# ScalarE's recurrence program without its loop, and the second extra piece of an attention step behind the values

## The reference, cut to what matters

```
# per expert e (4 of them), per sequence b (4), S = 512, D = 256, 16 heads of 16
q, k, v = split(h @ aiw + aib, 3)
attn = softmax(einsum('bhqd,bhkd->bhqk', q, k) * SCALE)       # 512 x 512 per head
h = einsum('bhqk,bhkd->bhqd', attn, v) ... @ aow + aob
hf = lstm(h, wif, whf, bf); hb = lstm(h[:, ::-1], ...)[:, ::-1]
# lstm, one step of 512:
zg = xt @ Wi + h @ Wh + b;  i, f, g, o = split(zg, 4)
c = sigmoid(f) * c + sigmoid(i) * tanh(g);  h = sigmoid(o) * tanh(c)
```

## Time and profile before

| | us |
|---|---|
| median of three runs | 5555.54 |
| the profiled execution | 5550.52 |
| its span | 5548.7 |
| TensorE busy | 5148.0 (93%) |
| VectorE busy | 4160.4 (75%) |
| ScalarE busy | 2497.2 (45%) |
| GpSimd busy | 1150.2 (21%) |
| attention steps, within the span | about 784 to 2130 |
| recurrence, within the span | about 2236 to 4990 |

### The profile page before, as it was taken

One profiled execution on the slowest core, in us unless ns is written; L12 is line 12 of the kernel. 1 busy time (PEld: TensorE's weight loads), 2 busy tenths in 40 slices (PEclk: granted clock), 3 DMA queues, 4 the chain that ended last, 5 costly groups with the idle time before them and its releaser, 6 DMA issues. The chain is left out here.

```text
span 5548.7 us, 260566 instructions
## 1 busy us (share of the span) xinstructions
PE 5148.0 (93%) x108704; PEld 3567.2 (64%) x108704; DVE 4160.4 (75%) x19277; ACT 2497.2 (45%) x8421; POOL 1150.2 (21%) x5133
## 2 busy tenths in 40 slices
PE   7888879999999997899999999999999999998895
PEld 4545433333333332888888888888888888884442
DVE  4555566666666664999999999999999999991224
ACT  2333446555555553444444444444444444443332
POOL 0000001111111110333333333333333333330000
PEclk9999989999999998999999999999999999999997
DMA  0003354444454443111101111011110111102110
GB/s 13 0 0 104 123 129 85 84 106 103 92 109 84 106 99 137 30 36 25 38 15 38 38 23 38 15 38 38 23 38 20 34 38 23 38 4 88 62 38 12
DMA packets 378077, 300.18 MB, mean 54 GB/s; under 512 B 145993, under 2 KB 357065, under 8 KB 372458
## 3 DMA queue, kind: packets, MB, share of 16 engines
q1 hardware_dynamic: 377886, 298.01, 22.5%
HBM read 178.94 MB, written 119.01 MB: 54 GB/s over the span
## 5 line engine op out<-in xcount | busy, mean ns | idle before, releaser
L1386 PE MATMUL bank<-lparts,lstate 128*32 128x256 bf16 x98304 | 2705.9, 273 | 95.3 <-PEq L1329 46.7
L1386 PEld LDWEIGHTS bank<-lparts,lstate 128*32 128x32 bf16 x98304 | 2455.2, 97 | 346.6 <-DVE lstate L1432 75.1
L1397 DVE STREAM_TRANSPOSE ltz<-bank 128x256 f32<-128x256 f32 x2048 | 920.5, 449 | 8.7 <-PE bank L1386 3.7
L1463 ACT ACTIVATE ltc<-lgc 128x16 f32<-128x16 f32 x2049 | 446.1, 218 | 1013.8 <-DVE lgc L1418 1013.4
L1479 POOL TENSOR_TENSOR wh<-lgate,ltc 128x16 f32<-128x16 f32 x2052 | 471.7, 230 | 1848.6 <-ACT ltc L1463 1777.4
L1114 DVE TENSOR_REDUCE bnegmax<-bank 128x1 f32<-128x512 f32 x1024 | 655.0, 684 | 218.4 <-PE bank L972 218.1
L1458 ACT ACTIVATE lgate<-lz 128x48 f32<-128x48 f32 x2048 | 502.0, 245 | 493.4 <-DVE lz L1408 493.0
L1202 ACT ACTIVATE wh<-bank 128x512 f32<-128x512 f32 x1024 | 554.3, 599 | 368.5 <-PE bank L990 368.2
L1486 POOL COPY ltz<-wh 128x64 f32<-128x64 f32 x2048 | 603.5, 295 | 0.0
L1404 DVE TENSOR_TENSOR lhalf<-ltz 128x128 f32<-128x128 f32 x2048 | 584.1, 285 | 5.0 <-POOL ltz L1486 5.0
L1052 PE MATMUL bank<-xT,bw 128*128 128x512 f32 x1024 | 487.4, 600 | 17.0 <-DVE bzs L1135 16.2
(11 more groups left out here) (211 smaller groups left out, 4712.2 us busy)
## 6 DMA issues: line engine op xcount, KB each, us to landing
zx<-bzs SPq DMA_DIRECT2D x32, 2048.0 KB, 7.3
wh<-zx SPq DMA_DIRECT2D x64, 1024.0 KB, 7.4
qk<-eparts SPq DMA_DIRECT2D x96, 256.0 KB, 2.6
bqp<-qk SPq DMA_DIRECT2D x192, 128.0 KB, 4.9
bkp<-qk SPq DMA_DIRECT2D x192, 128.0 KB, 8.0
hs<-wh SPq DMA_DIRECT2D x32, 512.0 KB, 5.7
cmemT<-hs SPq DMA_DIRECT2D x32, 512.0 KB, 4.2
vx<-evx SPq DMA_DIRECT2D x16, 544.0 KB, 3.7
```

Source lines behind the costliest of these rows:

```text
L1386: last = nc.tensor.matmul(bank[x][32 * q:32 * q + 32, 0:256], top[:, x, e, k].rearrange("p m r -> p (m r)"), parts[:, way, g, k, n, e, q], ...
L1397: nc.vector.transpose(tz[:, x].rearrange("p (n w) -> p n w", w=SLOT)[:, :, 0:32], bank[x][:, 0:256].rearrange("p (n c) -> p n c", n=BLOCKS ...
L1463: nc.scalar.activation(tc[:, x], gc[:, x, 1], ACT.Tanh).then_inc(tanhed[x], 1)
```

## The change

In the attention the second extra piece of a step moves from before `turn_maxima` and `values` to behind them, and `score_t(j - 2, 3)` now stands before `score(j, 3)`. In the recurrence ScalarE's loop over 32 turns of 16 steps is replaced by straight code for all 512 steps; the other engines' loops stay.

```diff
                     if j < HEADS:
                         score(j, 2)
-                        score(j, 3)
                     if 2 <= j < HEADS + 2:
                         score_t(j - 2, 3)
+                    if j < HEADS:
+                        score(j, 3)
+                    if 1 <= j < HEADS + 1:
+                        turn_maxima(j - 1)
+                    if j >= 6:
+                        values((j - 6) // 4, (j - 6) % 4)
                     if at == 0:
                         turn_values(slab, 0)
                     elif at == 1:
...
                     elif end > first + 1:
                         for k in range(KH):
                             product(made, end - 1, k)
-                    if 1 <= j < HEADS + 1:
-                        turn_maxima(j - 1)
-                    if j >= 6:
-                        values((j - 6) // 4, (j - 6) % 4)
...
-PE_STEPS, DVE_STEPS, ACT_STEPS = 4, 8, 16
+PE_STEPS, DVE_STEPS = 4, 8
...
-                with act.Fori(0, S // ACT_STEPS) as turn:
-                    first = ACT_STEPS * turn
-                    for i in range(ACT_STEPS):
-                        for x in range(chains):
-                            tanh_cell((x - 1) % chains, first + (i + (x - 1) // chains))
-                            gates(x, first + i)
+                for t in range(S):
+                    for x in range(chains):
+                        tanh_cell((x - 1) % chains, t + (x - 1) // chains)
+                        gates(x, t)
```

## The result

The changed kernel takes 5467.77 us (median of 4 runs, 5466.13 to 5469.04), the kernel before 5554.57 us (4 runs, 5552.78 to 5557.43): a ratio of 0.9843, 95% interval 0.9826 to 0.9860. That is 86.8 us, or 1.6%, less. The forecast was 5464 us in a range of 5446 to 5492, with 0.93 on faster. The profiled run took 5466.13 us and has a span of 5464.1.

A forecast was written before the change was run, and what follows sets the result against it. TensorE was taken to bound both stages, interrupted by waits on other engines. Attention 46 us plus recurrence 45 us made 91 us, taken from 5555.5 us for a forecast of 5464 us, range 5446 to 5492.

The forecast's parts named there:

- What bounds: Both stages: TensorE bounds attention (busy 1309 of 1346 us) and recurrence (2704 of 2754); the question is what interrupts it.
- ScalarE's turns, 31 at 1.65 us: Recurrence: each turn of ScalarE's 16-step loop costs 1.65 us, so removing 31 gives 51 us.
- GpSimd's turns come up, 6 us: Recurrence: GpSimd's seven late turns, formerly inside ScalarE's 1.65 us, remain and take 6 us (0 to 10) off the gain.
- VectorE's turns stay, 0.24 each: Recurrence: VectorE's 64 loop turns remain, each costing 0.24 us.
- ScalarE's code, nothing: Recurrence: 6144 activations as straight code need some 55 to 60 more instruction packets, fetched ahead and costed at nothing.
- The third rival: Recurrence: ScalarE waits for its straight code at some 55 packets, losing 242 us, kernel at 5707 us; chance 0.05.
- The second product, 0.40 us in each of 75 steps: Attention, two-product steps: the second product no longer waits for VectorE's keep of bank 7; 0.40 us each, 30 us.
- The price on the next step's first product, 0.06: Attention: the following step's first product may wait for VectorE's keep of the moved product, 0 to 0.11 us, taken as 0.06.
- The first rival: Attention: the wait moves to the next first product or a score; attention gains 24 us, kernel 5487 us; chance 0.14.
- The other second pieces, 10.5 + 7 - 1: Attention: second `turn_divided` gains 10.5 us, second `project` 7; `turn_values` and the first product's wait for the last projection take 1.
- The swap, nothing: Attention: exchanging the last two scores costs 0 or gives 0; VectorE still has the third block's maximum before the fourth.
- The sum: Whole kernel: attention 46 us plus recurrence 45 us, 91 us off 5555.5, forecast 5464 us.

The follow-up runs named there:

- e6: Changed kernel with ScalarE's recurrence loop of 16 steps back, its body beginning with the sigmoid so one table load stands in it: 5497.8 us (one run).
- e3: Changed kernel with ScalarE's recurrence program as a loop again, of 64 steps per turn: 5495.4 us, ratio 0.9895 to the kernel before.
- e10: e5 with GpSimd's recurrence loop also written out as straight code: 5452.3 us, ratio 0.9819 to the kernel before.
- e9: The changed kernel run again, unaltered, as a control on the same chip: 5466.6 us, ratio 0.9841 to the kernel before.
- e4: Changed kernel with the turned maxima between the values and the second piece in steps with a second extra piece: 5475.0 us, ratio 0.9857 to the kernel before.
- e5: Changed kernel with maxima and values directly behind the first product in two-product steps, the second product behind the wide scores: 5461.1 us, ratio 0.9827 to the kernel before.
- e8: Changed kernel without the move of the second pieces; the swap of the last score and last transposed score stays: 5507.3 us (one run).
- e2: Kernel before with only ScalarE's recurrence loop written out, attention as before: 5512.9 us, ratio 0.9924 to the kernel before.
- e7: Changed kernel with VectorE's recurrence loop written out as straight code too: 5462.1 us (one run).

## Why the prediction was right

*What bounds.* TensorE in both stages, with what interrupts it. Right: the gain is TensorE's idle time, 36.6 us of it in the attention (1408.10 - 1365.02 less 1367.60 - 1361.14), and 40 us in the recurrence (45.6 - 5.5). The total came right in part by luck: in the attention one term was too large and another left out, and they nearly cancelled.

*ScalarE's turns, 31 at 1.65 us.* Right in size. 64 slots away from GpSimd's turns take 84.40 us instead of 86.05, and e6 and e3 show that what costs is the loads with a body of 16 steps, and the loads with a halt of 2.3 us with one of 64. I had priced the turn as a whole and had not told loads and jump apart; the sum did not need it.

*GpSimd's turns come up, 6 us.* Right. TensorE is idle 0.63 to 0.98 us at each of the seven, 5.5 in all, and with GpSimd's loop written out 5.8 us of the recurrence go (e10 against e9).

*VectorE's turns stay, 0.24 each.* Right, in the changed kernel: its transposes at such a turn, as in the earlier trace rows, are 1.55, 1.23 and 1.39 us apart (they start at 2491.56, 2493.11, 2494.34 and 2495.73), 0.24 over three times 1.31.

The recurrence came to 2707.9 us where 2709 was said, a gain of 46.8 instead of 45.

*ScalarE's code, nothing.* Right. The packets went from 34 to 71 in 2000 us, 37 more; over the stage that is about 50, against the 55 to 60 estimated. ScalarE shows no wait without a semaphore. The third rival did not occur.

*The second product, 0.40 us in each of 75 steps.* This is the term that was too large. A pair of steps gained 0.33, which is 25 us instead of 30. I had counted the refill of 0.35 + 0.11 as all lost to the wait. The part behind the wait did go, but the moved product keeps 0.105 us of slow start with no wait at all: with narrow matmuls ahead its first weight load does not run ahead, as it had not behind the wait (e4, e5). The price on the next step's first product, 0.06, was 0.03 (1.75 instead of 1.72 in the rows of after; 4.80 against 4.73 for the step in which it lies includes this). The first rival named the next first product as the place where the gain would come back; it does so only by these hundredths.

*The other second pieces, 10.5 + 7 - 1.* Nearly right. A slab is 2.79 us shorter (86.83 to 84.04). Five pairs make 1.65 of it and the swap 0.19, so 0.95 are left for the tail, 14 us over 15 slabs, where 16.5 was said. Both named waits are gone, 10.3 us (the second `turn_divided`) and 9.3 us in the weight loads (the second `project`). The second `project` takes 1.82 us to the next row behind the values, and of its slow start nothing came back. The next first product now waits for the copy of the last projection in its weight loads, 4.4 us in 16 times (1.6, once, before). The terms were not taken apart by a run.

*The swap, nothing.* Wrong, though the total does not show it. The reason given was that VectorE has the third block's maximum before the fourth score. In steps in which no extra piece stands ahead of the third score it had not: TensorE waited for it 7.4 us in 35 times, 6.7 in 32 of them in the listing of the earlier trace rows. With the transposed score put between, the wait is gone, and e8 against e2 puts this at about 6 us.

*The sum.* The terms as stated make 46.5 + 45 = 91.5. Against them stand the second products' slow start (-5), the tail (-3, of which the ends of the attention are a part), the swap (+6), the lower clock at the beginning of the attention (-4), the recurrence (+2) and the rest of the program (-2.7). That leaves 85, and the spans differ by 84.6. At like clock the attention gained about 44 us of the 46 said, as 6 + 25 + 13 where the prediction had 0 + 30 + 16.5.

The Trainium skill's page "ScalarE: Activation LUTs", section "What ACT_TABLE_LOAD costs", has a load hold the engine 2.66 us. The rows of e3 speak against it as those of before did: a load starts at 2538.52, the activation 1.30 us later, and the next load at 2540.05. By the page's figure two loads per turn would have been an estimated 2.8 us longer; the turn was worth 1.66 us in all.

## What to carry to other kernels

Price a loop by what its body repeats (here two table loads) and by how long the body is, and look for another engine's turn in the same slots, which comes up next. Writing a loop out paid on ScalarE and GpSimd, which have idle time in each slot, and gave nothing on VectorE, which is busy nearly all the time. When a piece is moved to end a wait, look at the shape of its new neighbour too: behind narrow matmuls it kept 0.1 us that another place did not cost. Before two stages are compared, compare their clocks: the swap's 6 us were hidden in the profile by a lower clock at the beginning of the stage. And before a term is put at nothing, look for its row in the whole list of waits, small rows too.

## What the runs showed of the hardware

- A full-width f32 piece behind matmuls of 17 or 3 columns starts 0.105 us late (0.534 against 0.429 us between its first two matmuls). Behind a bf16 matmul of 128 columns it does so only where it had to wait. In both slow cases its first weight load begins with its first matmul, and in the quick one 0.22 us ahead. The Trainium skill's page "TensorEngine Tiling (Array Packing)", section "Key Properties", says that a change of the tiling mode drains TensorE. That could be the reason behind the narrow matmuls; it is not needed behind a wait, and no run here shows whether the mode or the width of the matmul ahead is what counts.
- A jump to the start of a long body halts the engine: 4.8 us on average on GpSimd (512 instructions), 2.25 to 2.46 on ScalarE (768), and not measurably on ScalarE with 192. Why fewer instructions cost GpSimd more is open.
- TensorE's granted clock fell to 1.2 GHz within its wait of 26 us ahead of the attention and stayed there for unequal times with equal programs: 30.7 us in the kernel before and 47.8 in e2, 47.8 us in the changed kernel and 41.0 in e9. The first slab took 54.0 us at 0.85 and 57.8 at 0.58. In e3 idle times of 0.65 to 1.00 and 2.71 to 3.17 us, one slot apart, came with 3.4 us at 1.2 GHz at four of seven turns and with none at three; each of the four cost 1.6 us more.
- Table loads belong to the body: a loop that begins with a tanh of one set and goes on with a sigmoid of another repeats both in each turn; begun with the sigmoid it repeats one, 1.23 us instead of 1.66 per turn; written out, none.
- VectorE's straight code costs as much as its loop of 8 steps: 11.7 us of late starts over 2048 slots against 13.5 us of turns (one run of e7).
